# A decoder layer with eight experts on one core: expert outputs gated in the tile and added onto the residual's rows by scattering DMAs, seven half tiles

## The chip, the cores and the metric

The kernel runs on one core of one Trainium2 chip. The metric is the device time of one execution in microseconds (us); lower is better.

## The reference

The input x has 32 batches of 128 rows (tokens) of 128 numbers, 4096 tokens in all, float32. The layer is

```
x = layernorm(x + self_attention(x))            # 16 heads of 8, scores times a decay
x = layernorm(x + cross_attention(x, ctx))      # a 128 x 128 gram matrix per batch, by head
x = layernorm(x + experts(x))

experts(x): xf = layernorm(x) * ln_g + ln_b
  logits = xf @ router_w                        # 8 experts
  scores, idx = top_k(logits, 2); gate = softmax(scores)
  per chosen expert e: y = layernorm(xf) * eg[e] + eb[e]
    x1 = y @ W1[e] + b1[e];  x2 = clip(y @ W2[e] + b2[e], -20, 20)
    h = clip(x1 * silu(x2), -1e4, 1e4)          # 512 wide
    out += gate * clip(h @ Wo[e] + bo[e], -1e4, 1e4)
```

Each token goes to two of eight experts, so there are 8192 rows of expert work.

## The kernel before

The instructions of every engine are written out by hand, with semaphores between engines. A wait (`wait_ge`, or `before` for one that can be trivial) stands ahead of its instruction, and everything behind them on that engine waits too. SyncE (SP) issues most DMAs, GpSimd (POOL) the indirect ones.

**Attention stage.** A loop over `s` from -2 to 32 is a software pipeline: in each step TensorE (PE), ScalarE (ACT), VectorE (DVE) and POOL do parts of up to eight batches. A batch ends with its routing: `norm2` (L1203) writes the residual of the last sum into `xall`, `best` and `best_index` find the two largest logits, `norm4` (L987) makes the normed row `xhat`, the ranks give each token two places in the DRAM buffer `expert_in`, and POOL's `scatter` (L469) writes `xhat` there with two indirect DMAs of 128 rows. A row carries 128 numbers, its own number and its first expert. The last nine batches are finished beside the expert tiles, by lists of what goes where: `beside(i, place)` on each engine, for step i.

**Expert stage.** There are 39 tiles of 256 rows (32 for 8192 rows, 7 for the experts' uneven counts); the first 15 (`FULL`) are planned from the counts of 23 batches, the other 24 by small operations on DVE in steps 10 to 12 (`late_*`). An expert step i has, on the engines:

- SP (`step`, from L299): the rows of tile i+2 (`xst`, L321), W2 and W1 of tile i+1 (L327, L328), Wo of tile i (L331); all are double buffers, each load waits until the tile before the last is done with its buffer. The three weights are 768 KB.
- PE: for each quarter c of the 512 hidden columns the up matmuls with W2 (L764) and W1 (L766) of tile i, then the down matmul (L785) of tile i-1; at c = 1 the two transposes (L799) of tile i+1.
- ACT: the bias of each quarter (L1021), silu of a half (L1027) in between, that of tile i-1 after the first bias; from tile 15 on three 128 x 128 diagonal matrices of gates per step (`diagonals`, L1008).
- DVE (`expert_step`): sum and clamp of the output of tile i-2 (`sum_y`, L1380, L1383), gated product and clamp of tile i-1's second half (`gate`, L1370, L1374), clip (L1363), `take_rows(i+1)` (L1391 to L1398: the expert's gain and offset onto the transposed rows, and the destination rows), product of tile i's first half, clip.
- POOL: the expert's parameters `prt` and `bot` of tile i+1 copied (L485, L488), then the scatter of tile i-2's output (L498) into the DRAM buffer `expert_out`, two indirect DMAs of 128 rows, each tile's after the landing of the one before.

**Last stage.** After the last landing SP loads both outputs of every token (4 MB, L337). PE sums per batch the residual and the two outputs through the diagonal gates (L872 to L874), DVE takes mean and variance (L1492, L1496), POOL the power -0.5 (L560, L562), ACT normalises (L1096), SP stores.

## Time and profile before

| | us |
|---|---|
| median of 3 runs | 637.29 (635.8 to 639.0) |
| the profiled execution, time / span | 634.83 / 633.1 |
| PE busy | 581.9 (92%) |
| DVE busy | 502.0 (79%) |
| ACT busy | 433.7 (69%) |
| POOL busy | 395.6 (62%) |
| attention stage, to the first up matmul of tile 0 | 349.5 |
| expert stage, to the last landing | 250.1 |
| last stage | 33.5 |

The span is what the trace covers, from the first instruction to the last; the time of the same execution is 1.7 us more. Busy shares are over the whole span, and stages differ, so a stage is read from the timelines and the windows inside it. Steps of the expert stage are named by the tile whose up matmuls PE does; a step lasts from the first of them to the first of the next tile.

### The profile page before, as it was taken

The page shows a single profiled execution, that of the slowest core. Times are in us where ns is not written, and L with a number is a line of the kernel's source. Part 1 is how long each engine was busy: PE and PEld are TensorE (multiplying, and loading weights), DVE is VectorE, ACT ScalarE, POOL GpSimd, SP SyncE. Part 2 cuts the span into 40 slices and gives each one's busy share as a digit, 9 for nine tenths or more (in the row PEclk, how much of TensorE's full clock was granted, in tenths as well). Part 3 has the DMA queues.
Part 4 walks back from the last instruction along what each step waited for, and adds up shares of the span by engine and source line. Part 5 has one row for each costly group of instructions (what it writes and reads, how often), then busy time and mean ns, then how long its engine had stood idle before and what let it go on. Part 6 is the DMA issues. An engine that isn't in the chain of part 4 may idle for free.

```text
span 633.1 us, 18345 instructions
## 1 busy us (share of the span) xinstructions
PE 581.9 (92%) x5275; PEld 464.5 (73%) x5275; DVE 502.0 (79%) x1508; ACT 433.7 (69%) x1179; POOL 395.6 (62%) x749
## 2 busy tenths in 40 slices
PE   3599999999999999999998789897999999999495
PEld 2266776777767777777766678786999899999395
DVE  1368899888898888988887677889888888888343
ACT  2267888888888888888867764445566676665234
POOL 2464558888788887878877565674444444444344
PEclk9999999999999999999989998999999999999889
DMA  3471212113121121221112454564655666665183
GB/s 96 125 109 43 67 36 75 51 57 75 51 74 56 56 74 51 72 59 51 41 35 60 136 158 127 158 194 142 197 191 179 181 186 200 190 180 162 54 295 93
DMA packets 69138, 70.22 MB, mean 111 GB/s; under 512 B 7184, under 2 KB 50256, under 8 KB 69040
## 3 DMA queue, kind: packets, MB, share of 16 engines
q1 hardware_dynamic: 62880, 57.28, 31.1%
q0 software_dynamic: 5392, 11.01, 5.5%
q8 instruction: 45, 0.74, 0.5%
q10 hardware_dynamic: 768, 0.75, 0.4%
q14 instruction: 53, 0.43, 0.2%
HBM read 53.85 MB, written 15.17 MB: 109 GB/s over the span
## 4 chain that ended last, share of the span: by engine, by line
PE 81%; DVE 6%; DMA 4%; issue 3%; ACT 2%; POOL 1%; SPq 1%; ACTq 0%; DVEq 0%; POOLq 0%
PE ps_s L713 11%; PE ps_t L724 9%; PE ps_m L785 9%; PE ps_a L735 6%; PE ps_s L764 5%; PE ps_t L764 5%; PE ps_s L766 5%; PE ps_t L766 4%; PE ps_a L744 4%; PE ps_m L641 2%; PE ps_m L697 2%; DMA expert_out<-yt,dest 2%; PE ps_m L608 1%; DVE hid L1370 1%; PE ps_m L689 1%
## 5 line engine op out<-in xcount | busy, mean ns | idle before, releaser
L498 POOL DMA_INDIRECT expert_out<-yt,dest x78 | 80.7, 1035 | 42.1 <-issue 25.0
L1121 DVE TENSOR_TENSOR sc<-ps_s,decay 128x512 f32<-128x512 f32 x128 | 84.7, 685 | 26.1 <-PE ps_s L713 25.8
L785 PEld LDWEIGHTS ps_m<-wot,hid 128*128 128x128 f32 x624 | 92.5, 191 | 16.8 <-DVE hid L1374 5.4
L785 PE MATMUL ps_m<-wot,hid 128*128 128x128 f32 x624 | 95.6, 276 | 5.4 <-DVE yt L1380 3.4
L879 ACT ACTIVATE pT<-ps_t 128x512 f32<-128x512 f32 x128 | 72.7, 593 | 17.0 <-PE ps_t L724 17.0
L713 PE MATMUL ps_s<-kbd,qT 32*128 32x512 f32 x256 | 75.9, 670 | 8.2 <-DMA kbd<-key_image 5.8
L724 PEld LDWEIGHTS ps_t<-ident,sc 128*128 128x128 f32 x512 | 57.3, 144 | 32.6 <-issue 30.4
L1132 DVE TENSOR_REDUCE rowmax<-sc 128x8 f32<-128x1024 f32 x64 | 78.1, 1220 | 0.4
L964 ACT ACTIVATE sc<-sc,rowmax 128x128 f32<-128x128 f32 x256 | 77.9, 390 | 0.0
L724 PE MATMUL ps_t<-ident,sc 128*128 128x128 f32 x512 | 77.1, 284 | 0.1
L469 POOL DMA_INDIRECT expert_in<-xhat,pos x64 | 65.2, 1018 | 16.3 <-issue 13.6
L1021 ACT ACTIVATE x2c<-ps_s,prt 128x256 f32<-128x256 f32 x78 | 37.0, 474 | 53.6 <-PE ps_s L766 53.6
L418 POOL TENSOR_TENSOR sc<-sc,rowmax 128x1024 f32<-128x1024 f32 x32 | 60.8, 1899 | 4.7 <-DVE rowmax L1132 4.6
L1021 ACT ACTIVATE x2c<-ps_t,prt 128x256 f32<-128x256 f32 x78 | 36.9, 473 | 36.4 <-PE ps_t L766 36.4
L764 PE MATMUL ps_s<-xg,w2t 128*128 128x256 f32 x156 | 49.7, 401 | 5.7 <-DVE hid L1370 4.1
L764 PE MATMUL ps_t<-xg,w2t 128*128 128x256 f32 x156 | 47.6, 387 | 4.7 <-DVE hid L1370 4.7
L488 POOL COPY bot<-bo_rows 128x128 f32 x39 | 12.2, 313 | 59.9 <-DVE yt L1380 59.9
L1027 ACT ACTIVATE sil<-x2c 128x512 f32<-128x512 f32 x78 | 48.4, 620 | 1.0 <-DVE x2c L1363 0.9
L735 PE MATMUL ps_a<-pT,vpad 128*32 128x128 f32 x1024 | 48.1, 285 | 0.0
L1370 DVE SCALAR_TENSOR_TENSOR hid<-ps_t,prt,sil 128x256 f32<-128x256 f32 x78 | 34.1, 479 | 16.6 <-ACT sil L1027 16.2
L766 PE MATMUL ps_s<-xg,w1t 128*128 128x256 f32 x156 | 46.7, 381 | 0.0
L766 PE MATMUL ps_t<-xg,w1t 128*128 128x256 f32 x156 | 46.4, 379 | 0.0
(261 smaller groups left out, 1431.8 us busy)
## 6 DMA issues: line engine op xcount, KB each, us to landing
w2t<-in_L_ffn_W_dram SPq DMA_DIRECT2D x39, 256.0 KB, 2.8
w1t<-in_L_ffn_W_dram SPq DMA_DIRECT2D x39, 256.0 KB, 3.1
wot<-in_L_ffn_Wo_dram SPq DMA_DIRECT2D x39, 256.0 KB, 3.7
kbd<-key_image SPq DMA_DIRECT2D x32, 256.0 KB
xst<-expert_in SPq DMA_DIRECT2D x39, 130.0 KB, 2.1
g<-expert_out SPq DMA_DIRECT2D x7, 512.0 KB, 8.5
key_image<-kT SPq DMA_DIRECT2D x32, 64.0 KB, 2.0
call<-in_ctx_dram SPq DMA_DIRECT2D x8, 256.0 KB, 6.7
```

The source lines that it names most:

```text
L498: pool.indirect_dma_start(ys_dram[:, :], bass.IndirectOffsetOnAxis(ap=dest[:, n, a:a + 1], axis=0), yt[:, par, a, :], None).then_inc(y_out ...
L713: mm = pe.matmul(ps_s[:, i, :, :], qT[rows, b % 3, :], kbd[rows, b % 3, :, :], start=True, stop=True)
L724: mm = pe.transpose(ps_t[:, i % 2, j * S:(j + 1) * S], sc[:, 2 * (b % 2) + i // 2, 4 * (i % 2) + j, :], ident[:, :])
L735: pe.matmul(mix_v[32 * j:32 * j + 32, :], vpad[:, b % 2, at:at + 32], pT[:, i, j * S:(j + 1) * S], start=i == 0, stop=i == GRP - 1)
L764: pe.matmul(ps_x2[c], w2t[:, par, P * c:P * c + P], xg[:, par, :], start=True, stop=True)
L766: pe.matmul(ps_x1[c], w1t[:, par, P * c:P * c + P], xg[:, par, :], start=True, stop=True).then_inc(up, 1)
L785: mm = pe.matmul(ps_y(i)[:, a * P:(a + 1) * P], hid[:, par, c, a * P:(a + 1) * P], wot[:, par, c, :], start=(c == 0 and a == 0), stop=(c = ...
L879: return act.activation(out, in_, ACT.Copy)
L964: done = act.activation(sc[:, slot, h, :], sc[:, slot, h, :], ACT.Exp, bias=rowmax[:, slot, h:h + 1])
L1021: act.activation(x2c[:, c, :], ps_x2[c], ACT.Identity, bias=prt[:, i % 3, 2 + CH + c:3 + CH + c]).then_inc(biased, 1)
L1121: dve.tensor_tensor(sc[:, 2 * (b % 2) + i // 2, j:j + 4, :], ps_s[:, i % 2, :, :], decay[:, :].unsqueeze(1).to_broadcast([P, 4, S]), ALU.m ...
L1132: dve.tensor_reduce(rowmax[:, slot, :], sc[:, slot], AX.X, ALU.max, negate=True).then_inc((maxed0, maxed1)[half], 1)
```

## The change

- Per batch ACT computes the gates from the two logits (`gates`) and DVE the reciprocal of their sum (`gate_inv`); the row written to `expert_in` carries both. So it has 132 numbers, and `scatter` also waits for the gates.
- DVE and POOL make a weight per row of a tile (`take_rows`, `weigh`), and ACT multiplies the tile's output by it (`gate_rows`), at the end of step i for tile i-2. POOL's scatter waits for that, and it adds (`compute_op=ALU.add`) onto rows of a DRAM buffer of one row per token.
- SP stores the residual of every batch into that buffer beforehand (`keep`), and POOL fills its spare rows.
- The last stage loads one row per token, 2 MB; PE, the diagonals and their gates go. POOL's power and DVE's shift are done in groups of four batches, not two.
- Of the 39 tiles, seven are 128 rows: from tile 18 on the kinds repeat full, full, half. Every instruction on a half tile is half as wide and the scatter is one DMA. The weights are loaded as before. The late tiles' table has two lists (full and half), with about ten more small DVE operations in steps 10 to 12, on 128 partitions instead of one; it also marks rows that a tile shares with another, and they go to spare rows.
- Three of POOL's `scatter` calls move from steps 7 to 9 to steps 9 and 10.

The late tables, widths that only follow `kind`, allocations and the constants are left out here.

```diff
-    RW = D + 2
+    RW = D + 4
...
+    FULLS = 2 * N // TILE
+    LATE = FULLS - FULL
+    kind = [2] * (FULL + LATE - 2 * (E - 1)) + [2, 2, 1] * (E - 1)
+    assert len(kind) == TILES and sum(kind) * P == 2 * N + (E - 1) * P
+    entry = [(0 if kind[n] == 2 else FULLS) + kind[:n].count(kind[n]) for n in range(TILES)]
...
-    ys_dram = nc.dram_tensor("expert_out", [2 * N + TILE, D], F32)
+    ys_dram = nc.dram_tensor("token_sum", [N + TILE, D], F32)
...
+                def keep(b):
+                    if b == EARLY:
+                        sp.wait_ge(kept, 16 * EARLY)
+                    sp.wait_ge(x2_ready, b + 1)
+                    sp.dma_start(ys_dram[0:N, :].rearrange("(p b) d -> p b d", p=P)[:, b, :], xall[:, b, :]).then_inc(kept, 16)
...
+                    if ever(b - 5):
+                        keep(b - 5)
...
+                for b in range(B - 5, B - 3):
+                    keep(b)
...
                         before(sp, aimed, n - 1)
-                        sp.dma_start(xst[:, par, :, :],
-                                     xs_dram[bass.ds(first, TILE), :].rearrange("(p a) d -> p a d", a=2)).then_inc(s_in[par], 16)
+                        before(sp, weighed, n - 1)
+                        sp.dma_start(xst[:, par, 0:kind[n], :],
+                                     xs_dram[bass.ds(first, P * kind[n]), :].rearrange("(p a) d -> p a d", a=kind[n])
+                                     ).then_inc(s_in[par], 16)
...
+                    if i == 1:
+                        keep(B - 3)
+                    if i == 5:
+                        keep(B - 2)
+                    if i == 8:
+                        keep(B - 1)
...
-                sp.wait_ge(y_out, 32 * TILES)
+                sp.wait_ge(y_out, outs(TILES))
+                sp.wait_ge(kept, 16 * B)
                 for i, (t, n) in enumerate(LOADS):
-                    sp.dma_start(g12[:, :, t:t + n, :],
-                                 ys_dram[0:2 * N, :].rearrange("(k p b) d -> p k b d", k=2, p=P)[:, :, t:t + n, :]
-                                 ).then_inc(got[i], 16)
+                    sp.dma_start(xall[:, t:t + n, :],
+                                 ys_dram[0:N, :].rearrange("(p b) d -> p b d", p=P)[:, t:t + n, :]).then_inc(got[i], 16)
...
                     pool.wait_ge(tagged, b + 1)
+                    pool.wait_ge(gate_ready, b + 1)
                     for k in range(2):
                         pool.indirect_dma_start(xs_dram[:, :], bass.IndirectOffsetOnAxis(ap=pos[:, b, k:k + 1], axis=0),
                                                 xhat[:, b, :], None).then_inc(scattered, 16)
+                def weigh(n):
+                    a = kind[n]
+                    pool.wait_ge(weighed0, n + 1)
+                    pool.tensor_tensor(weight[:, n, 0:a], weight[:, n, 0:a], xst[:, n % 2, 0:a, D + 3], ALU.mult).then_inc(weighed, 1)
...
                     beside(i, 1)
+                    if has(i, -1):
+                        weigh(i + 1)
                     if has(i, 2):
                         n = i - 2
-                        pool.wait_ge(y_ready, n + 1)
+                        pool.wait_ge(y_gated, n + 1)
                         pool.wait_ge(aimed, n + 1)
-                        before(pool, y_out, 32 * n)
-                        for a in range(2):
+                        if n == 0:
+                            pool.wait_ge(dumped, 16)
+                            pool.wait_ge(kept, 16 * EARLY)
+                        if n == FULL:
+                            pool.wait_ge(kept, 16 * B)
+                        before(pool, y_out, outs(n))
+                        for a in range(kind[n]):
                             pool.indirect_dma_start(ys_dram[:, :], bass.IndirectOffsetOnAxis(ap=dest[:, n, a:a + 1], axis=0),
-                                                    yt[:, par, a, :], None).then_inc(y_out, 16)
+                                                    yt[:, par, a, :], None, compute_op=ALU.add).then_inc(y_out, 16)
...
-                    if (i, place_) == (7, 2): scatter(B - 3); count(B - 2)
+                    if (i, place_) == (7, 2): count(B - 2)
                     if (i, place_) == (8, 1): choices(B - 1); tag(B - 1); place(B - 2)
-                    if (i, place_) == (8, 2): scatter(B - 2)
                     if (i, place_) == (9, 0): count(B - 1)
-                    if (i, place_) == (9, 2): place(B - 1); scatter(B - 1)
+                    if (i, place_) == (9, 1): scatter(B - 3)
+                    if (i, place_) == (9, 2): place(B - 1); scatter(B - 2)
+                    if (i, place_) == (10, 2): scatter(B - 1)
...
+                    w = P * kind[i]
+                    pe.matmul(ps_x2[c][:, 0:w], w2t[:, par, P * c:P * c + P],
+                              xg[:, par, 0:w], start=True, stop=True)
+                    pe.matmul(ps_x1[c][:, 0:w], w1t[:, par, P * c:P * c + P],
+                              xg[:, par, 0:w], start=True, stop=True).then_inc(up, 1)
...
-                pe.wait_ge(y_sum, TILES)
-                pe.wait_ge(spread, 1)
-                for i, (t0, n) in enumerate(LOADS):
-                    pe.wait_ge(got[i], 16)
-                    for t in range(t0, t0 + n):
-                        before(pe, fin_ready, t - 7)
-                        pe.matmul(sum_bank(t), ident[:, :], xall[:, t, :], start=True, stop=False)
-                        pe.matmul(sum_bank(t), diag[0][:, t, :], g12[:, 0, t, :], start=False, stop=False)
-                        pe.matmul(sum_bank(t), diag[1][:, t, :], g12[:, 1, t, :], start=False, stop=True).then_inc(summed, 1)
...
-                def diagonals(k):
...
-                def gate_exp():
-                    act.wait_ge(rt_gap, 1)
-                    act.activation(gate2[:, :], gate1[:, :], ACT.Exp).then_inc(rt_exp, 1)
+                def gates(b):
+                    act.wait_ge(top_ready, b + 1)
+                    before(act, gate_ready, b - 3)
+                    act.activation(xhat[:, b, D + 2:D + 4], top[:, b, 0:2], ACT.Exp, scale=-1.0, bias=top[:, b, 1:2],
+                                   accum_out=gsum2[:, b % 4:b % 4 + 1]).then_inc(gate_exp, 1)
+                def gate_rows(i):
+                    act.wait_ge(y_ready, i + 1)
+                    act.wait_ge(weighed, i + 1)
+                    for a in range(kind[i]):
+                        done = act.activation(yt[:, i % 2, a, :], yt[:, i % 2, a, :], ACT.Copy, scale=weight[:, i, a:a + 1])
+                    done.then_inc(y_gated, 1)
...
+                    if (i, place) == (8, 4): gates(B - 3); gates(B - 2); gates(B - 1)
...
-                        if i >= FULL:
-                            diagonals(i - FULL)
                         beside(i, 2)
                         bias(i, 2, par)
                         silu(i, 0)
                         beside(i, 3)
                         bias(i, 3, par)
                         beside(i, 4)
+                    if has(i, 2):
+                        gate_rows(i - 2)
...
+                    if ever(s - 7): gates(s - 7)
...
-                    act.activation(xall[:, t, :], sum_bank(t), ACT.Identity, bias=nm5[:, t:t + 1],
+                    act.wait_ge(nm5_ready, t // 4 + 1)
+                    act.activation(xall[:, t, :], xall[:, t, :], ACT.Identity, bias=nm5[:, t:t + 1],
                                    scale=rs5[:, t:t + 1]).then_inc(fin_ready, 1)
...
+                def gate_inv(b):
+                    dve.wait_ge(gate_exp, b + 1)
+                    dve.reciprocal(xhat[:, b, D + 3:D + 4], gsum2[:, b % 4:b % 4 + 1]).then_inc(gate_ready, 1)
...
-                    dve.tensor_scalar(xg[:, par, :], ps_x(n), prt[:, n % 3, 0:1], prt[:, n % 3, 1:2],
+                    a = kind[n]
+                    dve.tensor_scalar(xg[:, par, 0:a * P], ps_x(n)[:, 0:a * P], prt[:, n % 3, 0:1], prt[:, n % 3, 1:2],
                                       ALU.mult, ALU.add).then_inc(xg_ready, 1)
+                    dve.scalar_tensor_tensor(out=weight[:, n, 0:a], in0=xst[:, par, 0:a, D + 1], scalar=ecol[:, entry[n]:entry[n] + 1],
+                                             in1=xst[:, par, 0:a, D + 2], op0=ALU.is_equal, op1=ALU.max).then_inc(weighed0, 1)
+                    if n < FULL:
+                        dve.tensor_copy(dest[:, n, :], xst[:, par, :, D]).then_inc(aimed, 1)
+                        return
+                    if n == FULL:
+                        dve.wait_ge(row_nos, 4)
                     before(dve, aimed, n)
-                    dve.tensor_scalar(mine[:, :], xst[:, par, :, D + 1], ecol[:, n:n + 1], -float(N),
-                                      ALU.is_equal, ALU.mult).then_inc(own, 1)
-                    dve.wait_ge(own, n + 1)
-                    dve.tensor_tensor(dest[:, n, :], mine[:, :], xst[:, par, :, D], ALU.add).then_inc(aimed, 1)
+                    dve.scalar_tensor_tensor(out=mine[:, 0:a], in0=no_row[:, a - 1, 0:a], scalar=shared[:, entry[n]:entry[n] + 1],
+                                             in1=spare[:, a - 1, 0:a], op0=ALU.is_lt, op1=ALU.mult).then_inc(own, 1)
+                    dve.wait_ge(own, n - FULL + 1)
+                    dve.tensor_tensor(dest[:, n, 0:a], mine[:, 0:a], xst[:, par, 0:a, D], ALU.max).then_inc(aimed, 1)
...
-                    dve.wait_ge(summed, t + 1)
-                    dve.bn_stats(st5[:, t, :], sum_bank(t)).then_inc(stat5, 1)
+                    dve.wait_ge(got[0 if t < 2 else 1 if t < 4 else t // 4 + 1], 16)
+                    dve.bn_stats(st5[:, t, :], xall[:, t, :]).then_inc(stat5, 1)
...
-                for t in range(B + 4):
+                for t in range(B + 8):
                     if ever(t): last_stats(t)
                     if ever(t - 1): last_aggr(t - 1)
-                    if t % 2 == 1 and ever(t - 4): last_shift((t - 4) // 2)
+                    if t % 4 == 3 and ever(t - 7): last_shift((t - 7) // 4)
```

## Rows read from the trace of the kernel before

**Rows 1.** Windows view: start:end and length, busy us of each engine, PE clock, DMA.
```profile
200.00:300.00 100.00, 100.00 (x1178) 73.58 (x1177) 89.42 (x273) 85.97 (x261) 81.84 (x161) 1.00 0.20 60
...
349.50:443.10 93.60, 81.37 (x489) 71.60 (x489) 74.25 (x248) 52.84 (x108) 55.74 (x107) 0.98 0.51 154
443.10:556.07 112.97, 112.97 (x681) 101.90 (x681) 97.61 (x264) 74.36 (x175) 52.51 (x80) 1.00 0.61 188
...
599.60:633.10 33.50, 23.43 (x192) 23.27 (x192) 13.11 (x80) 12.76 (x32) 14.19 (x32) 0.86 0.58 189
```

**Rows 2.** Timeline of PE, one tile: start us, length us, engine, line, instruction.
```profile
556.07 0.67 PE L764 MATMUL ps_s<-xg,w2t 128*128 128x256 f32 x2
...
558.76 0.38 PE L799 MATMUL ps_a<-ident,xst 128*128 128x128 f32 x2
558.98 0.60 PE L764 MATMUL ps_t<-xg,w2t 128*128 128x256 f32 x2
...
560.29 0.60 PE L764 MATMUL ps_t<-xg,w2t 128*128 128x256 f32 x2
...
561.71 0.67 PE L764 MATMUL ps_s<-xg,w2t 128*128 128x256 f32 x2
```

**Rows 3.** Timeline of ACT, same tile.
```profile
557.26 0.47 ACT L1021 ACTIVATE x2c<-ps_s,prt 128x256 f32<-128x256 f32 x1 [1.06 <-PE ps_s L766]
557.63 0.62 ACT L1027 ACTIVATE sil<-x2c 128x512 f32<-128x512 f32 x1
...
561.36 0.47 ACT L1021 ACTIVATE x2c<-ps_t,prt 128x256 f32<-128x256 f32 x1 [0.32 <-PE ps_t L766]
```

**Rows 4.** Timeline of DVE, same tile.
```profile
557.48 0.29 DVE L1383 TENSOR_SCALAR yt<-yt 128x256 f32<-128x256 f32 x1
558.29 0.87 DVE L1370 SCALAR_TENSOR_TENSOR hid<-ps_t,prt,sil 128x256 f32<-128x256 f32 x2 [0.51 <-ACT sil L1027]
...
559.54 0.42 DVE L1363 TENSOR_SCALAR x2c<-x2c 128x512 f32<-128x512 f32 x1
559.87 0.54 DVE L1391 TENSOR_SCALAR xg<-ps_a,prt 128x256 f32<-128x256 f32 x1
560.33 0.45 DVE L1395 TENSOR_SCALAR mine<-xst,ecol 128x2 f32<-128x2 f32 x1
...
561.08 0.88 DVE L1370 SCALAR_TENSOR_TENSOR hid<-ps_s,prt,sil 128x256 f32<-128x256 f32 x2
```

**Rows 5.** Timeline of POOL, same tile.
```profile
558.37 0.97 POOL L498 DMA_INDIRECT expert_out<-yt,dest  x1 [0.44 <-issue]
559.64 1.16 POOL L498 DMA_INDIRECT expert_out<-yt,dest  x1 [0.31 <-issue]
560.81 0.22 POOL L485 COPY prt<-params 128x10 f32 x1
```

**Rows 6.** Groups by line and form, DVE then ACT, 345 to 592 us.
```profile
L1198 DVE SCALAR_TENSOR_TENSOR xc<-ps_m,mv,gain_row 128x128 f32<-128x128 f32 x3 | 0.9, 316 | 0.0
...
L1008 ACT ACTIVATE xhat<-ident,gate 128x128 f32<-128x128 f32 x32 | 12.5, 391 | 0.0
```

**Rows 7.** Chain that ended last, from 590 us: start us, length us, what.
```profile
593.06 2.25 DMA expert_out<-yt,dest
...
597.35 2.24 DMA expert_out<-yt,dest
599.61 2.81 DMA g<-expert_out
```

**Rows 8.** Timelines of ACT and DVE around the norm of the last batch.
```profile
388.51 0.47 ACT L1021 ACTIVATE x2c<-ps_t,prt 128x256 f32<-128x256 f32 x1 [1.21 <-PE ps_t L766]
...
390.54 0.40 DVE L1203 TENSOR_SCALAR xall<-ps_m,mv,rs 128x128 f32<-128x128 f32 x1
```

**Rows 9.** ACT at the end; POOL's sequencer on the kernel's last line.
```profile
627.53 1.22 ACT L1096 ACTIVATE xall<-ps_m,nm,rs 128x128 f32<-128x128 f32 x3
...
L259 POOLq DRAIN  x1: 5885/5885/5885, 627.0 to 627.0; - x1
```

251 lines of the change are left out of this document (134 added, 117 removed).

## The prediction

> **What bounds the kernel now.** I read the windows view first [rows 1]. The attention stretch (200 to 300 us) has TensorE (PE) busy all the time; so has the stretch of twenty expert tiles from 443.1 to 556.07, with VectorE (DVE) at 97.6 of 113.0 us and GpSimd (POOL) at 52.5. The last 33.5 us are unlike both: PE 23.4, DVE 13.1, and a DMA share of 0.58. "PE busy" hides a loop, so I next read the timelines of one expert tile on each engine, from 556.07 to 561.71 [rows 2]: the period is 5.64 us. PE's own work per tile is less: a quarter takes 1.31 us (558.98 to 560.29; the widths divide it into 0.87 for the up and 0.44 for the down matmuls), four make 5.24, and the two transposes 0.22, so 5.46. The rest is a loop over three engines. ScalarE (ACT) starts the bias of the first quarter 1.19 after PE [rows 3], then does the silu of the tile before; DVE starts the gated product when that ends, 1.03 after the bias's start [rows 4], then runs without a gap: product and clamp 1.25, clip 0.33, parameters onto the next rows 0.46, the two small operations for the destination 0.75, and the first quarter's product at 561.08, whose end lets PE start the next tile 0.63 later. 1.19+1.03+1.25+0.33+0.46+0.75+0.63 is 5.64: PE and the loop are within 0.2 us of each other. POOL is far from full, but it is in order: scatter, scatter, then the parameter copy for a later tile at 560.81 [rows 5].
>
> **Half tiles.** Seven of the 39 tiles become half as wide, each in a group full, full, half. PE does for a half tile half the up matmuls (4 x 0.44 instead of 4 x 0.87), and its down matmuls are interleaved into the next tile. The three tiles cost PE 2 x 5.46 + about 2.8 = 13.7, against 3 x 5.64 = 16.9 now. The loop shrinks less, for instructions have a fixed part: a DVE product of 128 x 128 takes 316 ns [rows 6] and one of 128 x 256 half of 0.87 us, a clamp of 256 elements 0.29 and of 512 0.42 [rows 4], an ACT operation of 128 elements 391 ns [rows 6] and of 256 0.47 [rows 3]. Into the loop: the step of the half tile is 0.75 (1.19 less half of 0.87) + 0.95 (a bias shorter by 0.08) + 1.25 + 0.21 + 0.46 + 0.55 + 0.49 = 4.66; the full tile behind it, which carries the half's second part, is 1.19 + 0.82 + 0.83 + 0.33 + 0.46 + 0.55 + 0.63 = 4.8; the other full tile, which prepares a half one, 5.64 - 0.16 - 0.2 = 5.3, so PE's 5.46 holds there. Sum 14.9 for the three; I take 15.0, so 1.9 saved, 13.5 over seven groups. The bounds are PE's 13.7 (22 saved) and 16.2 (5 saved), if what waits for weights or POOL eats two thirds. A half tile still loads 768 KB of weights. They are asked for when the up matmuls of the tile before the last are done, and have now 5.64 us to land and then 4.66; a load of the last stage lands in 2.8 [rows 7], so that should fit, with less to spare.
>
> **Small operations of a tile.** (The 0.55 above.) The weight (one more 128 x 2 operation) is new, the destination is made by a copy (early tiles), or by two operations without the scalar-times-constant form, which now takes 0.45 (560.33) [rows 4]. The 0.75 becomes 0.4 to 0.6: up to 0.2 per full tile until PE's 5.46 holds. For the five steady full tiles ahead of the groups I take 0.7 in sum. ACT gains two gate products per tile (2 x 0.3 to 0.39) and loses three diagonals per late tile; its idle microsecond before the next tile's bias covers them. If it did not, each would delay the loop by 0.3.
>
> **Scatter by adding.** Nothing in the trace adds in a DMA. A plain scatter's second half and its landing, until the next tile's second half is sent, take 597.35 - 593.06 = 4.29 us at the end, where only that chain runs [rows 7]; one scatter less saves 1.27 (558.37 to 559.64) [rows 5], so a half tile's cycle is 3.02. The adding one takes d more. Lower bound 0: nothing excludes that both reads overlap. Upper bound 2.2, the same way once more, if the old rows were fetched before anything else starts. It is nearest to the plain scatter, the same instruction with the same rows; I take 0.5. Then a full tile's cycle is 4.79 and a group's 2 x 4.79 + 3.52 = 13.1, hidden under 15.0. The cover goes at d = 1.2 for full tiles.
>
> What the row shows is a landing of 2.24 us for a scatter that reads once. The Trainium skill ("Collectives: The Full Stack", The bandwidth ceiling) says that an adding transfer is slower because it needs two source reads, on one ring, and halves the rate. By that rule the landing could double, and the whole kernel would take some 653; by the row it is 620. No row of this trace shows an adding DMA.
>
> **What is queued behind the new wait.** This is the change's cost. Now POOL scatters tile i-2 once DVE has summed it, 1.7 us into step i (557.48 + 0.29) [rows 4]. After, it waits for ACT's product, put behind the last bias of step i (561.36 + 0.47, then 0.6) [rows 3]: 6.4 us in, so in the next step. In the steady state the scatters then run from 1.0 to 3.4 us of the step, and the parameter copy ends near 3.65; DVE wants it at 3.80 (559.87). So nothing is lost, with 0.15 to spare. But in the first 13 tiles, where the last attention batches are still finished, POOL has more behind the scatter. In step 5 DVE does the last batch's second norm at 390.54 [rows 8], for which POOL has to raise a variance to a power first, behind step 4's scatters. After, tile 2's scatters wait for the product behind the bias of 388.51: start 389.6, end 392.1; two pairs of small operations (about 1 us each) follow, so 394.4, and DVE stands 3.9 us, with PE behind it. The same pattern follows: in step 6 the copy is queued behind two pairs of scatters (2 x 2.5 us), by my working 2.5 us late; in steps 9 and 10 POOL gets three and two pairs. I take 9 us for all, half of the 5 for the last absorbed by DVE's table work, which binds there already. Bounds: 0 (the stretch has waits today) and 14. The table work itself grows by some ten small operations of 0.17 and larger ones, about 1.5 us, and loses the gates' four (about 1): in the 9.
>
> **Attention.** Per batch ACT gains one exponential with its sum, DVE one reciprocal, SP one 64 KB store, which waits for a norm two batches old; spread_keys stands behind it. PE is busy throughout [rows 1], so all lie beside it: 0.5 in sum, 0 to 3.
>
> **End.** The last tile's chain: one scatter less (-1.3), a half tile's shorter latency (-1), ACT's product (+0.7), a later start of tile 37's scatters (+1.1), and d twice (+1.0): +0.5.
>
> **Last stage.** From the landing (599.6) to the end (633.1) it takes 33.5 us. The loads halve and the sums on PE (23.4 us, 0.73 per batch) go [rows 1]. What is late next: DVE is busy 13.1 us for 32 batches, 0.41 each [rows 1]; ACT's three norms in 1.22, 0.385 each [rows 9]. First load 2.8 [rows 7], then DVE needs eight batches and POOL one group before ACT's first norm: 6.2; 32 x 0.385 = 12.3; last norm to end, 4.35 (628.75 to 633.1). Sum 22.9: 10.6 saved, and POOL's drain of 5.9 us, which ends the kernel now [rows 9], gives 22.8 by its own way. I take 11 saved; bounds 8 and 14.
>
> **Sum.** The profiled execution took 634.83 (span 633.1). 634.8 + 0.5 + 9 - 0.7 - 13.5 + 0.5 - 11 = 619.6. The median of the runs, 637.29, is 0.4% above it; I forecast 620.
>
> **Rivals.** (a) The queue behind the product costs nothing: early steps last 7.2 us (93.6 / 13) and hide it. For: POOL is busy 55.7 of the 93.6 us of the first 13 steps [rows 1]; against: it is in order, and the 3.9 us come from its order, not its load. Then 611. (b) Half tiles don't pay: the loop, the weights or POOL's copy, which comes 0.15 us ahead of its use, hold a group at 16.2. Then 628. (c) The scatter chain becomes the bound, the way to slower. From tile 2 on (20 us after the first) POOL and the adding DMA go 32 x (4.29 + d) + 7 x (3.02 + d), plus 15 for the last batches' six pairs: 193 + 39 d, against 250 now from the first tile's start to the last landing. With 11 saved at the end it is slower than now from d = 1.73 on; at d = 2.2 it gives 634.8 + 29 - 11 = 653. For it: each scatter waits for the one before, and adding must read. Against: the scatter's 2.24 us hold 64 KB, which is 29 GB/s where the stretch before moved 188 [rows 1]; so most of them is latency, and a second read beside the first adds little to that.
>
> **How the numbers follow.** Forecast 0.46, (a) 0.19, (b) 0.18, (c) 0.17, of which 0.11 is beyond d = 1.73. Low end: half tiles at 18 and the last stage at 13, with (a): 604. High end: (b) and the mild part of (c): 638. A measurement of this kernel can tell about 0.5%, 3.2 us, from no change; so faster means under 634.1: 0.84; same 0.05; slower 0.11.
>
> **What would show it.** The last landing to the end in 22 to 25 us, no PE in it. A group of three near 15.0; if POOL's scatter is then released by the DMA each time, (c). DVE idle before the norm of the last batch for 3 to 4 us, released by POOL, and the parameter row waiting for the copy after it. Landing of the adding scatter 2.5 to 3.0. Wrong if the landing is over 3.5, or if full tiles take over 5.7.

## The result, and the profile after

The changed kernel takes 669.99 us (median of 4 runs, 668.5 to 673.0) against 637.58 for the kernel before on the same chip: 1.0516 times as long, 95% interval 1.0468 to 1.0564. It is slower; the forecast was 620, and the range ended at 638. One of e1_plain's eight runs below took 1335.59 us, in a slow state; its time and ratio are those of the other seven.

By the starts of the tiles' first up matmuls on PE, and the last landing, the profiled executions (spans 633.1 and 667.0 us) differ as follows:

| stage | before | after | difference |
|---|---|---|---|
| attention, to tile 0's first up matmul | 349.5 | 356.6 | +7.0 |
| first 13 steps (0 to 12) | 93.6 | 114.8 | +21.2 |
| five full steps (13 to 17) | 28.2 | 32.0 | +3.8 |
| steps 18 to 37 | 112.9 | 119.5 | +6.6 |
| tile 38's start to the last landing | 15.4 | 20.7 | +5.3 |
| last stage | 33.5 | 23.5 | -10.0 |

The forecast missed by 50 us. By its own terms some 20 are in the groups with half tiles (it had taken 13.5 off), 12 in the first 13 steps, 6.5 in the attention stage, 5 at the end, 4.5 in steps 13 to 17 and 1 in the last stage.

The windows view of the changed kernel, to be read beside [rows 1] (columns as there; the second row starts 0.1 us into step 18). The row of twenty tiles in [rows 1] is of steps 13 to 32; steps 18 to 37 of the kernel before give the same, PE 112.89 of 112.89 us and POOL 52.46:

```profile
356.56:471.37 114.81, 89.12 (x490) 76.80 (x490) 74.75 (x262) 59.85 (x139) 67.33 (x117) 0.93 0.50 127
503.40:622.82 119.42, 101.87 (x625) 89.11 (x626) 89.10 (x281) 64.00 (x156) 70.62 (x95) 1.00 0.70 170
643.55:667.00 23.45, 0.00 (x0) 0.00 (x0) 10.00 (x72) 13.17 (x32) 9.69 (x16) 0.50 0.58 179
330.00:340.00 10.00, 10.00 (x70) 7.43 (x70) 6.85 (x27) 4.27 (x12) 4.12 (x7) 0.50 0.07 20
```

In the second row PE is busy 101.9 of 119.4 us, where before it had no idle time. POOL, which was at 52.5, is at 70.6, though it has fewer scatters. The first line of POOL's groups shows the larger part of the reason (line, operation, count; busy us, mean ns; idle before, and who ended it):

```profile
L555 POOL DMA_INDIRECT token_sum<-yt,dest x71 | 115.6, 1628 | 82.3 <-ACT yt L1060 41.4 <-DMA token_sum<-yt,dest 28.1 <-issue 8.8
```

One adding scatter holds POOL for 1.63 us; the plain one had 0.97 to 1.16 [rows 5]. POOL's timeline at the end, where only the chain of scatters runs (start, length; idle before it and its releaser), and the chain's rows for the landings:

```profile
634.26 1.55 POOL L555 DMA_INDIRECT token_sum<-yt,dest  x1 [2.47 <-DMA token_sum<-yt,dest]
636.12 1.55 POOL L555 DMA_INDIRECT token_sum<-yt,dest  x1 [0.30 <-issue]
640.23 1.55 POOL L555 DMA_INDIRECT token_sum<-yt,dest  x1 [2.56 <-DMA token_sum<-yt,dest]
```

```profile
636.12 3.36 DMA token_sum<-yt,dest
640.23 3.31 DMA token_sum<-yt,dest
```

The second issue comes 1.86 us behind the first (1.27 before), the landing takes 3.36 (2.24 before, [rows 7]), and the next tile's first issue is 4.11 behind the last one (3.02 before). So a full tile's cycle is 1.86 + 4.11 = 5.97 us, not 4.29, and a half tile's 4.11, not 3.02: longer by 1.68 and 1.09.

The norm of the last batch, where the prediction saw the queue behind ACT's product, on DVE and on POOL:

```profile
397.79 0.34 DVE L1246 SCALAR_TENSOR_TENSOR xc<-ps_m,mv,gain_row 128x128 f32<-128x128 f32 x1
402.81 0.41 DVE L1251 TENSOR_SCALAR xall<-ps_m,mv,rs 128x128 f32<-128x128 f32 x1 [4.68 <-POOL rs L449]
```

```profile
397.52 1.58 POOL L555 DMA_INDIRECT token_sum<-yt,dest  x1 [2.28 <-ACT yt L1060]
399.40 1.55 POOL L555 DMA_INDIRECT token_sum<-yt,dest  x1 [0.30 <-issue]
...
401.82 0.18 POOL L447 TENSOR_TENSOR rs<-shift,mv 128x2 f32<-128x2 f32 x1
402.08 0.70 POOL L449 TENSOR_TENSOR rs<-rs,mhalf 128x2 f32<-128x2 f32 x1
```

POOL waits 2.28 us for the product, issues twice, and only then makes the power for which DVE stands idle for 4.68 us. That step takes 11.98 us (6.44 before), and the next, where the parameter copy is behind two pairs of scatters, 13.58 (7.33 before).

In the steady part POOL's loop reads:

```profile
540.88 1.58 POOL L555 DMA_INDIRECT token_sum<-yt,dest  x1 [1.75 <-ACT yt L1060]
542.77 1.57 POOL L555 DMA_INDIRECT token_sum<-yt,dest  x1 [0.30 <-issue]
543.76 0.79 POOL L535 COPY prt<-params 128x10 f32 x1
...
546.86 1.83 POOL L555 DMA_INDIRECT token_sum<-yt,dest  x1 [1.27 <-DMA token_sum<-yt,dest]
```

One scatter is released by ACT's product and the next by the landing: two limits lie close together, and the experiments take them apart. A group below is three tiles, full, full, half, from tile 18 on; its time is the mean of the first six. Before, three full tiles took 16.94.

### The profile page after: what moved, and what is told of

Its sections match the earlier page's. It is cut to its first block, busy times and chain, and to the rows that moved or that the text cites. A ratio compares the mean times of both kernels' runs of the same rounds, so it can differ in the third digit from the quotient of the medians.

```text
span 667.0 us, 18078 instructions
## 1 busy us (share of the span) xinstructions
PE 559.6 (84%) x5020; PEld 436.8 (65%) x5020; DVE 489.5 (73%) x1561; ACT 436.4 (65%) x1249; POOL 432.2 (65%) x775
## 4 chain that ended last, share of the span: by engine, by line
PE 53%; issue 16%; DVE 9%; DMA 8%; POOL 7%; ACT 4%; SPq 1%; POOLq 1%; ACTq 0%; DVEq 0%
PE ps_s L772 11%; PE ps_t L783 10%; PE ps_a L794 6%; DMA token_sum<-yt,dest 5%; POOL token_sum L555 5%; PE ps_a L803 4%; DVE hid L1441 3%; PE ps_m L700 2%; PE ps_m L844 2%; ACT sil L1075 2%; PE ps_m L756 1%; PE ps_m L667 1%; PE ps_m L748 1%; PE ps_m L693 1%; PE ps_m L686 1%
## 5 line engine op out<-in xcount | busy, mean ns | idle before, releaser
L555 POOL DMA_INDIRECT token_sum<-yt,dest x71 | 115.6, 1628 | 82.3 <-ACT yt L1060 41.4
L1068 ACT ACTIVATE x2c<-ps_t,prt 128x256 f32<-128x256 f32 (+1 forms) x78 | 35.4, 453 | 68.7 <-PE ps_t L826 68.1
L1068 ACT ACTIVATE x2c<-ps_s,prt 128x256 f32<-128x256 f32 (+1 forms) x78 | 35.4, 453 | 56.4 <-issue 37.9
L824 PE MATMUL ps_s<-xg,w2t 128*128 128x256 f32 (+1 forms) x156 | 46.9, 383 | 29.5 <-DVE hid L1441 27.6
L824 PE MATMUL ps_t<-xg,w2t 128*128 128x256 f32 (+1 forms) x156 | 47.5, 387 | 9.6 <-DVE hid L1441 9.6
L1464 DVE TENSOR_SCALAR xg<-ps_a,prt 128x256 f32<-128x256 f32 (+1 forms) x38 | 19.6, 517 | 37.8 <-issue 36.5
L1075 ACT ACTIVATE sil<-x2c 128x512 f32<-128x512 f32 (+1 forms) x78 | 45.5, 583 | 1.1 <-DVE x2c L1433 1.1
L824 PEld LDWEIGHTS ps_s<-xg,w2t 128*128 128x128 f32 x156 | 23.7, 192 | 34.2 <-issue 30.2
L1441 DVE SCALAR_TENSOR_TENSOR hid<-ps_t,prt,sil 128x256 f32<-128x256 f32 (+1 forms) x78 | 32.3, 455 | 18.4 <-ACT sil L1075 18.0
L826 PE MATMUL ps_t<-xg,w1t 128*128 128x256 f32 (+1 forms) x156 | 45.6, 375 | 0.0
```

What stands on the lines that cost most here:

```text
L555: pool.indirect_dma_start(ys_dram[:, :], bass.IndirectOffsetOnAxis(ap=dest[:, n, a:a + 1], axis=0), yt[:, par, a, :], None, compute_op=ALU ...
L824: pe.matmul(ps_x2[c][:, 0:w], w2t[:, par, P * c:P * c + P], xg[:, par, 0:w], start=True, stop=True)
L1068: act.activation(x2c[:, c, 0:w], ps_x2[c][:, 0:w], ACT.Identity, bias=prt[:, i % 3, 2 + CH + c:3 + CH + c]).then_inc(biased, 1)
```

## Experiments

Theory A: the adding DMA's longer cycle binds the steady part, and the late product, with POOL's small operations behind the scatters, binds the first 13 steps. The rivals in each expectation are other places for the same loss. Ratios are to the kernel before on the same chip; stage times are from profiled executions.

**e1_plain**: in the changed kernel

```diff
-   yt[:, par, a, :], None, compute_op=ALU.add).then_inc(y_out, 16)
+   yt[:, par, a, :], None).then_inc(y_out, 16)
```

> The changed kernel with a plain scatter in place of the adding one; every row keeps the last output written to it, so the residual and one expert's part are missing from the sums. Theory A (the adding DMA itself is the cause: in the changed kernel its issue takes 1.60 us on POOL against 0.98, and at the end a half tile's cycle is 4.11 against 3.02): 617 to 630 us, a group of full, full, half at 15.0 to 15.5 instead of 17.8. Theory B (the queue behind ACT's product is the cause): 650 or more, a group still over 17. Both in part: 635 to 648.

640.19 us, 1.0068 (1.0039 to 1.0097). Of the 5.2% that the change costs, 4.5 points (28 us) go with the adding: both causes in part, nearer to the adding. Full steps 13 to 17 are back at 28.2 us, groups at 16.4 (not the 15.0 to 15.5 of theory A), but the first 13 steps still last 106.7, and the norm of the last batch still waits:

```profile
397.47 0.41 DVE L1251 TENSOR_SCALAR xall<-ps_m,mv,rs 128x128 f32<-128x128 f32 x1 [3.46 <-POOL rs L449]
```

**e2_early**: in the changed kernel, on ACT

```diff
                         bias(i, 1, par)
+                    if has(i, 2):
+                        gate_rows(i - 2)
+                    if has(i, 0):
                         beside(i, 2)
...
                         beside(i, 4)
-                    if has(i, 2):
-                        gate_rows(i - 2)
```

> The changed kernel with ACT's gate products of tile i-2 placed after the second bias of step i instead of after the last, some 3 us earlier in the step. Theory A (the adding DMA): the scatters still follow each other at 5.97 us for a full and 4.11 for a half tile, so a group can't fall under 16.05; 655 to 668. Theory B (the queue behind the product): the parameter copy comes 3 us earlier, and most of the 33 us go: 640 or less.

656.28 us in two runs, 1.0313 (1.0258 to 1.0368): 13 us less. The first 13 steps fall from 114.8 to 105.1 and the norm's wait from 4.68 to 1.96 us. The groups stay at 17.85 us, where the changed kernel has 17.84: with the product early, all 20 tiles' scatters of steps 18 to 37 wait for landings, and theory A's other cause keeps the steady part. The waits in that stretch (who waited for what; us in total, times, longest):

```profile
POOL token_sum L555 <- DMA token_sum<-yt,dest: 29.6, 20, 2.0
DVE xg L1465 <- issue: 16.7, 14, 1.9
```

The second line has no releaser, but the timelines do: DVE takes the next rows 0.1 us after the parameter copy has ended, which stands behind the scatters on POOL.

**e3_halves**: the kernel before, with `kind`, half-wide instructions and the two-list table alone; output, gates and last stage as before.

```diff
+    kind = [2] * (FULL + LATE - 2 * (E - 1)) + [2, 2, 1] * (E - 1)
...
-                        for a in range(2):
+                        for a in range(kind[n]):
```

> The kernel before with the seven half tiles and their tables alone; gates, scatter, last stage as before. Forecast of the half tiles: a group at 15.0 instead of 16.9, so 13.5 less than before: 622 to 626 against 637. Rival b (half tiles don't pay): 631 to 638, a group at 16.2 or more.

627.20 us, 0.9856 (0.9807 to 0.9905), faster than both, and between the two expectations. Groups take 15.60 us; the regular ones 5.57 + 4.57 + 5.21 = 15.35. The first 13 steps take 95.6 us, 2.0 more than before.

**e4_add**: the kernel before, with only the adding.

```diff
+                    if 6 <= b < 22:
...
+                        sp.dma_start(flat[:, (b - 6) * w:(b - 5) * w], zrow[:, :]).then_inc(blank, 16)
...
-   yt[:, par, a, :], None).then_inc(y_out, 16)
+   yt[:, par, a, :], None, compute_op=ALU.add).then_inc(y_out, 16)
```

> The kernel before with nothing but the adding scatter: 16 stores of zeros blank the buffer during attention, and rows that two tiles share are counted twice in it. Theory A: the cycle of scatters of a full tile is 5.97 us against the 5.64 of PE, 0.3 more on each of the 26 steady tiles and 1 to 2 on the 11 steps that also scatter inputs: 650 to 665. Theory B (adding is hidden, the order is the cause): 637 to 642.

660.05 us in two runs, 1.0372 (1.0316 to 1.0429). Rows that two tiles share count twice in its output. Here is no product, no gate and no half tile, and steps 18 to 35 take 6.18 us in the mean instead of 5.65. Of the 24.6 us that the profiled execution is longer, 13.9 lie in steps 13 to 37 and 9.3 behind the start of tile 38; the first 13 steps lose 2.8, and not the 1 to 2 each that theory A had put on eleven steps. POOL, two tiles:

```profile
503.24 1.56 POOL L504 DMA_INDIRECT expert_out<-yt,dest  x1 [2.64 <-DMA expert_out<-yt,dest]
505.11 1.75 POOL L504 DMA_INDIRECT expert_out<-yt,dest  x1 [0.31 <-DVE hid L1376]
...
509.21 1.56 POOL L504 DMA_INDIRECT expert_out<-yt,dest  x1 [1.90 <-DMA expert_out<-yt,dest]
```

From issue to issue 5.97 us, the figure of the changed kernel's end. The chain alone is enough for a slower kernel.

**e5_plain_early**: the edits of e1_plain and e2_early together.

> The changed kernel with plain scatters in place of the adding ones, and with ACT's product of tile i-2 moved up to stand right behind the second bias of step i (it leaves the sums out, so the output lacks the residual and one expert's part). Theory A (two causes: the adding DMA's longer cycle, and in the first 13 steps POOL's queue standing behind ACT's late product): the first 13 steps come back from 106.7 us to 95-99, groups of three stay near 16, last stage 23.5, so 628 to 633 in all. Rival (the loss that is left with plain scatters in the first 13 steps comes from the three moved scatter calls and the larger table, not from the product's place): the first 13 steps stay over 103 us and the time over 636.

633.07 us, 0.9899 (0.9825 to 0.9973). With plain scatters the product's place is worth 1.7 points, with an interval of 0.9 to 2.5; the two profiled executions differ by 5.5 us. The first 13 steps come to 102.8 us: 4 of the 13 us lost there. That is the rival's 103 rather than theory A's 95 to 99, though the total is at the upper end of theory A's range and the rival's 636 is not reached.

**e6_two_buffers**: the changed kernel, odd tiles into a second buffer.

```diff
-                        before(pool, y_out, outs(n))
+                        before(pool, y_out[par], outs(n, par))
...
-   pool.indirect_dma_start(ys_dram[:, :], ...
+   pool.indirect_dma_start((ys_dram, odd_dram)[par][:, :], ...
```

> The changed kernel with adding scatters, but odd tiles add into a second buffer of the same size (cleared by nine stores during the attention stage and not read at the end), so that a tile's scatters wait for the landing of the tile before the last only. The output lacks the odd tiles' part. Issue on POOL stays at 1.6 us each, landing stays as long. Theory A (it is the chain issue, issue, landing, next tile that binds): full tiles after the 13th step back to 5.6-5.7 us, groups 15.6-16.5, last landing earlier by 15 or more, 640 to 652 in all (the first 13 steps keep part of their loss, for POOL is still held 1.3 us longer per tile). Rival (the longer hold of POOL by the issue binds, through the parameter copy behind it): groups stay at 17.5 or more, time over 660.

655.71 us, 1.0265 (1.0186 to 1.0343): between the two expectations. The end comes back (20.7 to 16.2 us from tile 38's start to the last landing), the groups only to 16.74, and the first 13 steps not at all (117.9). POOL waits for the product now, and the loop that goes through both binds:

```profile
527.77 1.58 POOL L563 DMA_INDIRECT odd_sum<-yt,dest  x1 [1.25 <-ACT yt L1070]
529.66 1.70 POOL L563 DMA_INDIRECT odd_sum<-yt,dest  x1 [0.30 <-issue]
530.64 0.93 POOL L542 COPY prt<-params 128x10 f32 x1
```

```profile
531.67 0.41 DVE L1474 TENSOR_SCALAR xg<-ps_a,prt 128x128 f32<-128x128 f32 x1 [0.39 <-issue]
...
532.45 0.88 DVE L1451 SCALAR_TENSOR_TENSOR hid<-ps_s,prt,sil 128x256 f32<-128x256 f32 x2
```

The copy ends at 531.57, DVE takes the next rows at 531.67, and the product that lets PE start the next tile follows at 532.45. The prediction had left this loop 0.15 us of room with issues of 0.98; two longer ones use it up, and steps 15 to 18 are 6.0 to 6.2 us.

**e7_half_rows**: e4_add with rows of 64 numbers into a buffer that is not read; every output lacks the experts' part.

```diff
-   pool.indirect_dma_start(ys_dram[:, :], ... yt[:, par, a, :], ...
+   pool.indirect_dma_start(half_dram[:, :], ... yt[:, par, a, 0:D // 2], ...
```

> The kernel before with adding scatters as in e4_add, but of rows of 64 numbers (256 B) into a buffer of its own, which is not read at the end; half of every output is left out. If the adding DMA's price goes by rows: issue 1.55-1.60 us, landing to the next tile's issue unchanged within 0.2 us, full steps 6.1-6.2, time 650 to 662. If it goes by bytes: the landing shorter by 0.5 us or more, steps under 5.8, time under 648.

657.88 us in its one run; steps 18 to 35 take 6.02 us in the mean, a little under the 6.1 expected. Issue 1.57 us in the median, as in e4_add. The landings (five in e4_add's chain, 3.28 to 3.41 us, mean 3.33; seven here, mean 3.19) are 0.15 us shorter with half the bytes:

```profile
602.76 3.29 DMA expert_half<-yt,dest
608.66 3.27 DMA expert_half<-yt,dest
614.54 3.11 DMA expert_half<-yt,dest
```

So the price does not go by bytes. Whether it goes by rows or by the DMA was not taken apart: every scatter has 128 rows. The page's row of POOL's DMA queue (packets, MB, share of the 16 engines) shows more packets for adding, not more bytes; for before, e4_add and e7_half_rows:

```profile
q0 software_dynamic: 5392, 11.01, 5.5%
```

```profile
q0 software_dynamic: 14128, 11.01, 11.2%
```

```profile
q0 software_dynamic: 14128, 8.46, 9.3%
```

14128 - 5392 over 78 scatters are 112 packets more for each adding DMA of 128 rows.

**e9_two_early**: e6_two_buffers with e2_early's edit.

> e6_two_buffers (adding scatters, odd tiles into a second buffer that is not read, each tile waits for the landing of the tile before the last) with ACT's product of tile i-2 moved up behind the second bias of step i. Alone, the early product left the groups of three at 17.85 us (e2_early) and the second buffer at 16.74 (e6_two_buffers). Theory: two limits of nearly one size, the chain of landings and the loop product, two issues of 1.6 us, parameter copy, hid; so only both together free the step: full tiles after the 13th step 5.6-5.7 us, groups as with plain scatters, 15.8-16.5, the first 13 steps near e2_early's 105, 636 to 645 in all. Rival (the longer issue costs time wherever it stands on POOL, or the adding traffic slows the weights' loads): groups stay at 16.7 or more, full tiles over 6.0, time over 648.

634.28 us, 0.9972 (0.9941 to 1.0004), a little under the expectation: 3.4 points under e2_early, 2.9 under e6_two_buffers. Groups 15.96, steps 13 to 17 29.0, the first 13 steps 107.2. In the groups the two limits were of nearly one size: lifting the one alone gave nothing (17.85), the other alone 1.1 us (16.74), both 1.9. In the totals the gains of 2.0 and 2.5 points alone and 5.4 together are not clear of a plain sum. POOL's issues are as long as ever, and little waits for them (from 487 to 594 us DVE waits for the parameter copy 5 times, 1.9 us in all):

```profile
520.23 1.59 POOL L563 DMA_INDIRECT odd_sum<-yt,dest  x1 [0.51 <-issue]
522.12 1.57 POOL L563 DMA_INDIRECT odd_sum<-yt,dest  x1 [0.30 <-issue]
523.11 0.79 POOL L542 COPY prt<-params 128x10 f32 x1
```

**e10_order**: the changed kernel with POOL's order turned round from step 3 on.

```diff
...
                     if has(i, -1):
                         weigh(i + 1)
+                    if i >= AHEAD:
+                        beside(i, 2)
+                        beside(i + 1, 0)
+                        if has(i, -2):
+                            copy_prt(i + 2)
                     if has(i, 2):
...
-                    beside(i, 2)
+                    if i < AHEAD: beside(i, 2)
```

> The changed kernel, all of it, with only POOL's order changed: from step 3 on the last batches' operations behind tile i-2's scatters, those at the start of step i+1 and the parameter copy of tile i+2 stand ahead of the scatters and not behind them. Theory (in the first 13 steps VectorE waits for small POOL operations that are queued behind two issues of 1.6 us and the late product): the first 13 steps come back from 114.8 us to 97-104; groups of three stay at 17.5-18 because the chain of landings binds them still; 653 to 661 in all. Rival (the first 13 steps are long for the moved scatters of expert_in, the gates' activation-table loads and the larger table): they stay over 108 and the time over 664.

652.96 us, 1.0249 (1.0191 to 1.0308). The first 13 steps come back from 114.8 to 103.9 us; steps 5 and 6 take 6.32 and 7.71 us, not 11.98 and 13.58. The norm that waited 4.68 us has no idle time in front of it (groups 17.34, a little under what was expected):

```profile
397.32 0.34 DVE L1261 SCALAR_TENSOR_TENSOR xc<-ps_m,mv,gain_row 128x128 f32<-128x128 f32 x1
397.60 0.41 DVE L1266 TENSOR_SCALAR xall<-ps_m,mv,rs 128x128 f32<-128x128 f32 x1
```

**e12_order_early**: both repairs of order, e10_order and e2_early, with one buffer.

> The changed kernel, all of it and computing the whole reference, with both repairs of order: ACT's product behind the second bias (as in e2_early, 656.3 us) and POOL's small operations and parameter copy ahead of the scatters (as in e10_order, 653.0 us). What is left is one buffer, in which each tile's adding scatters wait for the landing of the tile before. Theory: the first 13 steps a little under e10_order's 103.9 (99-103), but groups of three stay at 17.2-17.9 because only the chain of landings sets them; 646 to 653 in all, so the change stays slower than the kernel before by 1.5% or more in its best order. Rival (the chain can be hidden once POOL is free): groups under 16.7, time under 641.

649.37 us, 1.0221 (1.0156 to 1.0285), as expected; the first 13 steps, 104.4, miss their 99 to 103 and are no better than e10_order's. Groups 17.17; the scatters are released by the landing:

```profile
529.40 1.74 POOL L570 DMA_INDIRECT token_sum<-yt,dest  x1 [1.55 <-DMA token_sum<-yt,dest]
531.44 1.55 POOL L570 DMA_INDIRECT token_sum<-yt,dest  x1 [0.30 <-issue]
...
535.54 1.59 POOL L570 DMA_INDIRECT token_sum<-yt,dest  x1 [1.68 <-DMA token_sum<-yt,dest]
```

The parameter copy is ahead of them now, so the landing reaches PE by another way: DVE may write a tile's output only when the scatters of the tile before the last, whose buffer it is, have landed, and it waits for that 19 times in steps 18 to 37:

```profile
DVE yt L1468 <- DMA token_sum<-yt,dest: 16.6, 19, 2.0
```

With one buffer the change stays slower than the kernel before in both orders, alone and together.

**e8_halves_warm, e11_halves_last**: e3_halves with its end changed; e8_halves_warm has the first loop alone, e11_halves_last has 18 in place of 34 and the second loop too, and leaves that matmul out later for these eight batches.

```diff
                 pe.wait_ge(y_sum, TILES)
+                for _ in range(34):
+                    pe.matmul(sum_bank(7), ident[:, :], xall[:, 0, :], start=True, stop=True)
+                for t in range(8):
+                    pe.matmul(sum_bank(t), ident[:, :], xall[:, t, :], start=True, stop=False)
```

> e3_halves (the kernel before with half tiles and tables alone) with 34 matmuls on PE between the last expert tile and the first load of the last stage, whose result nobody reads. In e3_halves PE has 7 us of idle there and then runs its first nine batches at a granted clock of 0.50 (1.28 us per batch against 0.67 later). If the idle stretch is what lowers the clock: the first batches take 0.67 us each, last stage 30-31 us instead of 33.8, time 623 to 625. Rival (the last stage waits for its loads then, or the clock stays low): 626 to 628.

> e3_halves with the end changed: between the last expert tile and the first load PE runs 18 idle matmuls and then the residual's matmul of the first eight batches, whose banks are free, so that eight batches need two matmuls and not three behind the load. e8_halves_warm, with idle matmuls alone, had its last stage in 31.8 us against 33.8. If PE still sets the pace behind the loads: 8 x 0.22 less, last stage 29.5-30.5 us, time 0.4 to 0.8% under e3_halves (623 to 626 where before has 636). Rival (the loads are behind PE then, so that nothing more is to be had): last stage 31.5-32.

629.42 us, 0.9854 (0.9796 to 0.9913), and 625.57 us, 0.9826 (0.9787 to 0.9865); neither can be told from e3_halves, and the first is beyond both its expectations. In e3_halves PE idles while the last tile's output lands and the first load comes (8.38 us, not the 7 of the expectation), and then has this clock (timeline, windows, e3_halves):

```profile
594.66 0.77 PE L895 MATMUL ps_s<-xall,ident 128*128 128x128 f32 x2 [8.38 <-DMA g<-expert_out]
595.00:600.00 5.00, 5.00 (x25) 5.00 (x25) 1.06 (x5) 0.00 (x0) 0.51 (x2) 0.50 0.98 342
600.00:605.00 5.00, 5.00 (x45) 5.00 (x45) 2.80 (x18) 1.83 (x5) 2.98 (x7) 0.97 1.04 387
```

In e8_halves_warm the granted clock is 1.00 in every stretch from 585 to 615 us and the last stage takes 31.8 us instead of 33.8, where 30 to 31 were expected. In e11_halves_last PE is ready sooner than the loads and idles between them, and the clock falls again:

```profile
590.00:595.00 5.00, 4.19 (x34) 3.66 (x32) 1.44 (x7) 0.00 (x0) 0.24 (x2) 1.00 0.85 260
595.00:600.00 5.00, 3.52 (x22) 3.53 (x23) 1.61 (x10) 1.28 (x4) 2.45 (x5) 0.79 1.01 356
```

Its last stage is 33.4 us, beyond the rival's 31.5 to 32 too; the rival's reason, the loads, fits the DMA share of 1.01.

## Why the prediction was wrong

**The scatter by adding (0.5 us for d, and 0 for the issue): the step that failed.** The prediction took the adding scatter as a plain one whose landing may be longer, so d counted the landing alone and the issue stayed at 0.98 us. Both grew: the issue to 1.57 us, the landing from 2.24 to 3.36, a cycle of 5.97 us for a full and 4.11 for a half tile. d is 1.68 for a full tile and 1.09 for a half one, inside the bounds of 0 and 2.2 but past 1.2, where by the prediction's own working the cover goes. "Nearest to the plain scatter" was the wrong reason for 0.5: the trace had no row for the thing that differs. e4_add, whose expert part differs in nothing else, shows it: +3.7%. The prediction's own sign of being wrong, full tiles over 5.7 us, came true.

The landing is 3.36 / 2.24 = 1.5 times the plain one's. The Trainium skill ("Collectives: The Full Stack", The bandwidth ceiling) says, of large transfers in a ring, that adding needs two source reads and halves the rate; the direction is right, the factor for this small scatter is less than its two, and e7_half_rows, which halves the bytes and changes the landing by 0.15 us, does not look like a rate. What the rule led to, 653 us, was nearer to 670 than the forecast.

**Rival (c), the scatter chain as the bound (0.17): right in kind, too cheap.** At d = 1.68 its formula gives 193 + 66 = 259 us from tile 0's start to the last landing and a kernel near 632; measured are 287 us. Its price was taken at the kernel's end, where only the chain runs, and the groups take 17.84 us where 2 x 5.97 + 4.11 is 16.05. The landings are longer beside the tiles' loads; from issue to landing, steps 18 to 37 of the kernel before, the changed one and e1_plain:

```profile
DMA to landing us min/median/max: 2.2/2.4/3.5
DMA to landing us min/median/max: 3.2/3.9/5.8
DMA to landing us min/median/max: 2.3/3.4/6.0
```

In e2_early, where only landings release these scatters, a tile's first issue comes 4.53 us behind the last one of the tile before (mean of tiles 19 to 36), not 4.11. 3 x 4.53 + 2 x 1.86 = 17.3 us is most of what its groups take. Why the landings are longer there is not shown. The rival also had no term for longer issues in the first 13 steps.

**The queue behind the product (+9; bounds 0 to 14): the mechanism right, the size open.** With plain scatters DVE's wait for the last batch's norm is 3.46 us against 3.9 forecast. The first 13 steps lose 13.1 us there (e1_plain), but the product's early place brings back only 3.9 of them (e5_plain_early), so that the 9 is not confirmed: most of the loss was still there. With the longer issues these steps lose 21.2 us; e10_order, which changes POOL's order alone, brings 10.9 of them back. That shows the mechanism and refutes rival (a), by which it costs nothing. "In the steady state nothing is lost, with 0.15 to spare" holds with plain scatters (steps 13 to 17 take 5.63 each in e1_plain) and fails with adding ones (6.0 to 6.2 in e6_two_buffers).

**Half tiles (-13.5): right in kind, smaller, and hidden.** e3_halves has 15.35 for a regular group and 15.60 in the mean against 15.0 forecast, and gains 9 us (1.4%), its larger table included. In the changed kernel the group is 17.84, bound elsewhere. Rival (b), 16.2 a group, is refuted for e3_halves.

**Small operations (-0.7): no gain.** Steps 13 to 17 take 28.2 us before and in e1_plain, though the operation with a scalar and a constant is gone.

**Attention (+0.5; 0 to 3): half right.** Of the +7.0, 2.5 lie ahead of the first batch, and e3_halves, whose attention stage is that of before, has 2.8 there. From the first batch's norm to tile 0 seven kernels with the change's attention stage (e1_plain, e2_early, e5_plain_early, e6_two_buffers, e9_two_early, e10_order, e12_order_early) take 287.9 us in the mean, and six without it (before, e3_halves, e4_add, e7_half_rows, e8_halves_warm, e11_halves_last) 286.1: +1.8. The changed kernel's own 291.7 has in it ten microseconds at a granted clock of 0.50 (330 to 340, above), where e1_plain has 0.83 and e2_early 1.00.

**End (+0.5): +5.3.** With plain scatters it is +1.1 (e1_plain, 16.4 us); the rest, 4.3, is about what three longer cycles make, 2 x 1.68 + 1.09.

**Last stage (-11; 8 to 14): the number right, by luck in part.** 23.5 us, forecast 22.9, measured gain 10.0. The start is as forecast: the first norm 6.29 us behind the landing, against 6.2. But ACT does not set the pace. It does four norms in 1.65 every 1.85 us and waits 0.2 each time for DVE's shift, which waits for POOL's power:

```profile
649.84 1.65 ACT L1144 ACTIVATE xall<-xall,nm,rs 128x128 f32<-128x128 f32 x4 [15.24 <-DVE nm L1582]
651.70 1.65 ACT L1144 ACTIVATE xall<-xall,nm,rs 128x128 f32<-128x128 f32 x4 [0.21 <-DVE nm L1582]
```

```profile
650.45 1.01 POOL L621 TENSOR_TENSOR rs<-rs,mhalf 128x4 f32<-128x4 f32 x1
651.50 0.16 DVE L1582 SCALAR_TENSOR_TENSOR nm<-mv,rs 128x4 f32<-128x4 f32 x1 [0.63 <-POOL rs L621]
```

DVE does the fourth batch's statistics behind the shift, and POOL waits 0.56 us for those: the loop through DVE and POOL binds. So the 32 norms take 14.4 us and not 12.3, and a shorter way from the last norm to the end, 2.8 us instead of 4.35, makes up for it.

**The range** ended at 638 because only "the mild part" of (c) was let in. The chance of 0.84 for faster rested on one price that no row showed.

**What stays open.** With both repairs or with plain scatters the first 13 steps still take 103 to 107 us against 93.6 before (e3_halves: 95.6, of which the larger table is part). The moved scatters of the last batches, the late gates and the longer steps 0 and 3 are candidates; they were not taken apart. Nor was it shown why with plain scatters the groups are at 16.4 and not at e3_halves' 15.60; a plain scatter's landing there is 3.4 us in the median, where before it was 2.4. Why an adding DMA's issue is longer is not shown either: that POOL has more packets to describe is an inference from the queue's row. The Trainium skill ("DMA: Bandwidth & Descriptors", SWDGE vs HWDGE vs iDMA) says that for DMAs issued from GpSimd a program on that engine computes the descriptors, which would fit; no run here shows it apart.

## What to carry to other kernels

An operation that no row shows should be priced with all its parts, its issue on the engine's queue as well as its landing, and where cover goes inside the bounds, the forecast must be made for both sides of that point. A wait should be priced under the load that it will meet: the landing of 3.3 us at the end was 3.9 in the steady part. When an in-order engine is given a later wait and a longer instruction at once, look for a second limit of nearly the same size: here, lifting the one alone left a group at 17.85 us, the other alone gave 16.74, and both together 15.96. The gain of the change lay in its half tiles and its short last stage; scattering by adding into one buffer cost more than both, and half tiles alone make the kernel 1.4% faster.

## What the runs showed of the hardware that was not expected

- An indirect DMA that adds 128 rows of 512 B holds POOL for 1.57 us in the median (e4_add, 78 of them, 1.55 to 1.90) instead of 0.98 (before, 0.96 to 1.19), lands in 3.3 to 3.4 us instead of 2.25 where little else moves and in 3.9 instead of 2.4 (medians) in steps 18 to 37, and leaves 112 packets more on its queue. With rows of 256 B the issue and the packets are the same, and the landing at the end is 0.15 us shorter.
- The small POOL operations directly behind an adding scatter are shown with 0.78 us and more (the copies above) where behind a plain one they have 0.22 [rows 5]; the copy's record begins before the scatter's ends (543.76 against 544.34 above), so only some 0.2 us of the copy's 0.79 is time added.
- The granted clock was 0.50 (1.2 GHz) for some 6 us when PE began again behind 8.4 us of idle time in e3_halves, stayed at 1.00 (2.4 GHz) when matmuls without use filled that time, and was 0.79 in a stretch in which PE idled 1.5 us in 5 for its loads.
